# Edge means: TensorE reads a round's ten block numbers as two packed words of ready offsets

## The reference, cut to what matters

```python
count = zeros(N); total = zeros((N, 16))
count[dst] += 1                      # edges that arrive at each node
total[dst] += edge_attr_16           # their 16 attributes, summed
mean16 = total / maximum(count, 1)   # used by the second graph layer
dinv = 1 / sqrt(count + 1)           # used by the third graph layer
```

## Time and profile before

| what | value |
| --- | --- |
| time, median of 3 runs | 6425.63 us (6424.36 to 6426.48) |
| time of the profiled execution | 6432.7 us |
| its span | 6431.1 us |
| first to last read of block numbers in the stage | 1952.3 us to 2158.5 us of the span, 22 reads |
| granted TensorE clock, whole span | 0.899 |

### The profile page before, as it was taken

One profiled execution on the slowest core, in us unless ns is written; L12 is line 12 of the kernel. 1 busy time (PEld: TensorE's weight loads), 2 busy tenths in 40 slices (PEclk: granted clock), 3 DMA queues, 4 the chain that ended last, 5 costly groups with the idle time before them and its releaser, 6 DMA issues. The chain is left out here.

```text
span 6431.1 us, 120342 instructions
## 1 busy us (share of the span) xinstructions
PE 4931.8 (77%) x25586; PEld 3714.0 (58%) x25587; DVE 4307.1 (67%) x13252; ACT 2765.0 (43%) x8055; POOL 3078.3 (48%) x3493
## 2 busy tenths in 40 slices
PE   5621999994574578888883899969989997888685
PEld 4510777763453356666663566645657775666575
DVE  7770888873785679999996777753433335888612
ACT  0010877773114336666662111124523333877423
POOL 4786777776473048888880222213310001777221
PEclk9975999997695689999995999979999998999698
DMA  6522444455585222222231555543520002666453
GB/s 237 179 65 58 122 121 124 119 112 104 142 250 147 61 59 69 69 68 70 67 67 49 170 181 188 184 127 106 154 79 10 10 10 60 160 160 159 75 170 118
DMA packets 843340, 719.85 MB, mean 112 GB/s; under 512 B 405662, under 2 KB 749251, under 8 KB 842660
## 3 DMA queue, kind: packets, MB, share of 16 engines
q1 hardware_dynamic: 596280, 372.06, 20.3%
q0 software_dynamic: 120064, 280.26, 16.4%
q10 hardware_dynamic: 126828, 65.67, 3.5%
HBM read 521.19 MB, written 201.60 MB: 112 GB/s over the span
## 5 line engine op out<-in xcount | busy, mean ns | idle before, releaser
L1054 POOL DMA_INDIRECT l3e_rows<-table,l3e_idx x440 | 437.4, 994 | 736.6 <-DVE l3e_idx L1076 608.3
L1054 POOL DMA_INDIRECT l0e_rows<-table,l0e_idx x440 | 446.9, 1016 | 149.9 <-issue 132.0
L1054 POOL DMA_INDIRECT l1e_rows<-table,l1e_idx x440 | 429.1, 975 | 121.4 <-issue 121.4
L3366 ACT ACTIVATE l1e_weighted<-l1e_rows,l1e_power 128x64 f32<-128x64 f32 x1760 | 462.9, 334 | 16.7 <-ACT l1e_power L3357 9.3
L824 POOL DMA_INDIRECT records_by_src<-l0n_rec_src,l0n_pos_at_src x390 | 398.1, 1021 | 115.4 <-issue 108.8
L1331 PE MATMUL l0e_ps_w<-l0e_wf,l0e_hidT 128*128 128x256 f32 x1760 | 415.8, 390 | 34.5 <-DVE l0e_shifted L1272 34.3
L1331 PEld LDWEIGHTS l0e_ps_w<-l0e_wf,l0e_hidT 128*128 128x128 f32 x1760 | 330.3, 193 | 161.9 <-issue 88.4
L3307 PE MATMUL l1e_ps_row<-net_ident,l1e_logit 128*128 128x128 f32 x1760 | 276.9, 280 | 127.5 <-DVE l1e_logit L3502 126.4
L2673 ACT ACTIVATE l1fg_hT<-l1fg_ps_h,l1fg_b_cols 128x256 f32<-128x256 f32 x256 | 107.3, 470 | 530.6 <-PE l1fg_ps_h L2616 530.6
L2055 ACT ACTIVATE l2fe_hT<-l2fe_ps_h,l2fe_own,l2fe_own 128x320 f32<-128x320 f32 x320 | 197.5, 617 | 310.1 <-PE l2fe_ps_h L2005 309.8
L3321 PE MATMUL l3e_ps_s<-l3e_weighted,l3e_onehot 128*128 128x257 f32 x880 | 253.0, 433 | 93.0 <-ACT l3e_weighted L3368 92.9
(11 more groups left out here) (833 smaller groups left out, 14858.8 us busy)
## 6 DMA issues: line engine op xcount, KB each, us to landing
counts<-l1f_total ACTq DMA_DIRECT2D x272, 128.0 KB, 4.0
l1fg_w_in<-in_L_ffn_W SPq DMA_DIRECT2D x32, 1024.0 KB
l1fg_w_out<-in_L_ffn_W SPq DMA_DIRECT2D x32, 1024.0 KB
records_by_dst<-l0n_blank_dst SPq DMA_DIRECT2D x5, 6512.0 KB
l3e_rec<-records_by_dst SPq DMA_DIRECT2D x110, 296.0 KB, 3.2
l2d_counts<-counts SPq DMA_DIRECT2D x208, 128.0 KB, 2.4
l2d_counts<-counts POOLq DMA_DIRECT2D x192, 128.0 KB, 2.7
l3fg_w_in<-in_L_ffn_w SPq DMA_DIRECT2D x16, 1024.0 KB, 7.2
```

The lines of the kernel that those rows point to most:

```text
L1054: pool.indirect_dma_start(at(self.rows[b], k, self.width), None, self.table, bass.IndirectOffsetOnAxis(self.idx[b][:, k:k + 1], 0)).then_i ...
L3366: act.activation(out[:, h, 0:each], g.rows[b][:, lo:lo + each], ACT.Copy, scale=power[b][:, m * heads + h:m * heads + h + 1])
```

## The change

At the end of setup VectorE packs the block numbers five to a word, five bits each, and shifts each word left by six bits, so that a field read in place is already the number times 64, the column at which the block's sums begin. There are 44 such words, in `round_word_dst`. TensorE reads two words at the head of a round in place of ten numbers, tests the two against bounds, and takes each field out with a shift and a mask ahead of the pair's matmuls (with a mask alone for the first field of a word). The matmuls and their operands are the same.

```diff
+FIELDS, FIELD_BITS, SUMS_BITS = 5, 5, 6
...
+        self.round_word = None if weighted else s.sb(f"round_word_{key}", [P, PAIRS // FIELDS], I32)
...
         link(dve.tensor_copy(to.block_row[:, :], t["pair_blk"]))
+        word, fields = to.round_word[:, :], to.block_row[:, :].rearrange("p (w n) -> p w n", n=FIELDS)
+        link(dve.tensor_copy(word, fields[:, :, FIELDS - 1]))
+        for n in reversed(range(FIELDS - 1)):
+            link(dve.tensor_single_scalar(word, word, FIELD_BITS, op=ALU.logical_shift_left))
+            link(dve.tensor_tensor(word, word, fields[:, :, n], ALU.bitwise_or))
+        link(dve.tensor_single_scalar(word, word, SUMS_BITS, op=ALU.logical_shift_left))
...
-def blocks_of_round(net, engine, placed, first, n):
-
-    _, blocks = net.nc.values_load_multi_w_load_instructions(placed.block_row[0:1, bass.ds(first, n)], engines=[engine],
-                                                             min_val=0, max_val=NT - 1)
-    return blocks
+def offsets_of_round(net, engine, placed, rnd):
+
+    n = RING * TWO // FIELDS
+    top = ((NT - 1) * ((1 << FIELD_BITS * FIELDS) - 1) // ((1 << FIELD_BITS) - 1)) << SUMS_BITS
+    _, words = net.nc.values_load_multi_w_load_instructions(placed.round_word[0:1, bass.ds(rnd * n, n)], engines=[engine],
+                                                            min_val=0, max_val=top)
+    mask = ((1 << FIELD_BITS) - 1) << SUMS_BITS
+    return [(word >> (FIELD_BITS * m)) & mask for word in words for m in range(FIELDS)]
...
                 if b == 0:
-                    of_round[:] = blocks_of_round(net, mybir.EngineType.PE, placed, q * TWO, RING * TWO)
-                blocks = of_round[b * TWO:(b + 1) * TWO]
+                    of_round[:] = offsets_of_round(net, mybir.EngineType.PE, placed, i)
+                offsets = of_round[b * TWO:(b + 1) * TWO]
...
-                    pe.matmul(at(ps, blocks[k // 2], W)[:, 0:SUMS], at(onehot[b], k, P),
+                    pe.matmul(ps[:, bass.ds(offsets[k // 2], SUMS)], at(onehot[b], k, P),
```

More of the change, by code:

```diff
@@ L2941, in combine_and_means @@
     TILE = 16 + 9 * 16
-    SUMS, W = 49, 64
+    SUMS, W = 49, 1 << SUMS_BITS
     TWO_TILES = NT // 2
```

## The result

The median of four runs after is 6377.18 us (6372.94 to 6379.6), against 6426.06 us (6424.36 to 6437.09) for four runs before: a ratio of 0.9913, with an interval of 0.9901 to 0.9925. The forecast was 6368.5 us, with a range of 6358 to 6390. The profiled execution after took 6377.27 us, with a span of 6375.6 us and a granted clock of 0.902.

The account below looks back on a forecast made before the run. TensorE's sequencer at each round's head was taken as the bound. 21 rounds go from 206.2 to 9 × 6.9 + 12 × 7.05 = 146.7 us; less 0.9 and 1.5, net 57.1 off 6425.6 gives 6368.5 us, range 6358 to 6390.

Parts of the forecast that it names:

- The read: At TensorE's round head, reading two words in place of ten numbers takes 0.55 us, saving 1.33 us a round.
- The forecast's lower end: Lowest price for reading two words at the round's head: 0.30 us plus the short reads' slope of 0.09, 0.39 us.
- The tests: At TensorE's round head, eight fewer run-time bounds tests at 0.287 us each save 2.30 us a round.
- The register operations: On TensorE, 18 added operations a round to take out fields cost 93 ns each, 1.67 us a round.
- Rival 3: Operations taking out fields cost only 50 ns each; early rounds fall to SyncE's 6.3 us; 6362 us or less; chance 0.14.
- rival 4: Operations feeding a matmul's address cost more, turning point about 0.26 us each; at 0.30 us, 6446 us; chance 0.03.
- The round: TensorE's steps from start of sums to start of sums add to 6.79 us, 6.87 with the data chain.
- What is late next: After TensorE's head shrinks, the data chain sets early rounds at 6.9 us; VectorE's additions nearly set late ones, 7.05 us.
- VectorE's floor: In the last 12 rounds, VectorE's `last` steps and additions to `x` allow no round shorter than 6.96 us.
- The wait for the expert rows: Ten rounds in, VectorE waits for GpSimd's last fetch before its additions begin: +1.5 us once.
- Rival 2: Record loads into the stage become the limit, a round some 8 us: 36 us saved, 6390 us; chance 0.10.
- the first round: Filled by start-up, its read hidden but its register operations not wholly: +0.9 us once.

## Why the prediction was right, point by point

**The read.** 0.55 us forecast from "two times 0.27", 0.558 measured. The reason given was right for the wrong half: long reads do go word by word, at 0.27 us each (2.74 / 10). Short ones don't, and the runs show why: 0.85 us for twelve words is three steps of 0.28, and 1.08 for ten is two such steps and two single words, (2 + 2) × 0.27. An aligned read thus seems to take four words at a step and what is left one by one. Two words then make no group of four and go one by one from either address, which is why the forecast's price held: partly by luck, as it had the words of every read go so. Those three lengths and 0.30 for a single word fit this, and the 0.81 us expected for twelve words was worked out from it before the run; other lengths and other offsets weren't tried. The forecast's lower end, by the slope of the short reads, is not borne out. The Trainium skill ("Runtime: NRT & Kernel Launch", Instruction fetch mechanics) says about 200 ns a register, even in bulk. It says so of registers filled from HBM, and the reads here are of SBUF. The runs go from 0.07 us a word (twelve, aligned) to 0.27 (unaligned) and 0.30 (a single one), so its figure agrees here only with the mean over the kernel before, 0.19.

**The tests.** 0.287 us each: 2.30 us a round forecast for eight. In the changed kernel the two tests of a round still begin 0.286 us apart. The kernel without any of the ten shortened its rounds by 2.4 of 2.87 us, and there the late rounds with a short read stop at 6.82 us, near VectorE's own limit (below). Two tests fewer after the change took 0.5 of 0.57 us off the early rounds. The price stands.

**The register operations.** 0.093 us forecast, 0.096 in the trace, 0.07 to 0.09 as what ten more added. The same section of the Trainium skill names an issue floor of some 20 cycles an instruction, an estimated 17 ns at the prediction's 1.2 GHz. The row of 32 to 36 ns alone is twice that. A floor is a lower bound and no price, so the trace does not contradict it, as the prediction had it do. Rival 3 (50 ns each) is out, as is rival 4 (0.26 us).

**The round.** Term by term: head 2.63 forecast and 2.63 measured, then 1.12 and 1.11, 1.01 and 1.12, 0.92 and 0.98, 1.11 and 1.11. The sum was 6.87 and is 6.95; the mean of the early rounds is 7.05. That two terms agree to the last digit is luck in part: six neighbouring heads take 2.62 to 2.77 us.

**What is late next.** 7.05 us was forecast for late rounds and 7.08 measured, but "VectorE's floor, 4 × 0.99 + 3.00 = 6.96" was put together wrongly. The 0.99 was itself set by TensorE and ScalarE. Where VectorE has a backlog its step is 0.95 (2031.41 to 2032.36, 2033.30). In a late round of both kernels with ready offsets the five steps of `last` are 0.96, three of 0.94 and 2.98, 6.76 us in all, with nothing left to wait for: that is VectorE's floor. In most late rounds of the changed kernel they are some 0.96, 0.94, 1.03, 1.17 and 2.99, so VectorE waits ahead of two of them. The 7.08 is a longer loop, seen in this stretch of the changed kernel:

```profile
2071.86 2.12 DVE L3113 SCALAR_TENSOR_TENSOR net_x<-means_out,l0f_weight,net_x  x4
...
2073.91 0.29 DVE L3106 TENSOR_TENSOR means_parts<-means_rest,means_parts 128x128 bf16<-128x128 f32 x1
...
2074.63 0.47 PE L3050 MATMUL means_ps<-means_parts,means_onehot 128*128 128x49 bf16 x4
...
2075.58 0.60 PE L3050 MATMUL means_ps<-means_parts,means_onehot 128*128 128x49 bf16 x4
...
2076.87 0.60 ACT L3080 ACTIVATE means_partsT<-means_ps_t 128x512 bf16<-128x512 bf16 x1
...
2077.36 0.35 ACT L3069 ACTIVATE means_parts<-means_rec 128x192 bf16<-128x192 f32 x1
2077.62 0.35 ACT L3073 ACTIVATE means_parts<-means_rest 128x192 bf16<-128x192 f32 x1
...
2078.00 0.29 DVE L3106 TENSOR_TENSOR means_parts<-means_rest,means_parts 128x128 bf16<-128x128 f32 x1
...
2078.95 0.48 DVE L3113 SCALAR_TENSOR_TENSOR net_x<-means_out,l0f_weight,net_x  x1
```

VectorE's additions make `last` late (2073.91); TensorE's third batch waits for it, and does this and the next batch with their register operations (2074.63, 2075.58); its transposes release ScalarE's `keep` (2076.87), behind which stand `first` and `second`; these release `last` (2078.00), and one `hot` later the next additions begin. The loop passes two batches of TensorE but not the round's head. It is read from these rows, and three runs bear it out: removing the head's tests leaves 7.08, taking the register operations away gives 6.76, and moving the additions gives TensorE's own 6.95. With ten more register operations TensorE's own round, 6.95 + 10 × 0.093 = 7.88 us, is the longer of the two limits again, against 7.78 measured.

**Once only.** The wait for the expert rows was to cost 1.5 us; it cost 1.6 in the profiled run and 3.6 in the next. It is the term with the largest scatter. GpSimd's last fetch was issued 67.0 us after the first in the profiled run and 69.4 in the next, where it was 65.3 before. The kernels with aligned and with shifted rows, whose rounds are longer, took 71.6 and 67.4 us on that chip, so the difference is not shown to come from the change. The two stretches of the earlier trace rows in the changed kernel:

```profile
1967.40:2030.40 63.00, 44.55 (x360) 26.49 (x360) 45.68 (x133) 47.14 (x136) 47.31 (x45) 0.52 0.90 216
2030.40:2120.20 89.80, 63.38 (x505) 38.00 (x506) 81.91 (x234) 65.99 (x184) 0.00 (x0) 0.50 0.53 120
```

The DMA share in the early rounds is 0.90, where it was 0.61, with 216 GB/s for 147. Rival 2 had this for a limit. VectorE's wait for the records grew only from 2.7 us to 4.4, and ScalarE's from 11.3 to 11.8, so it did not take hold. It may be what makes the early rounds 7.05 us and not 6.95: on the third chip, where the fetches end before the third round and the share is 0.56 behind it, the early rounds take 6.93. No run on one chip separates this. TensorE's granted clock is 0.52 and 0.50, the 1.2 GHz level, as before.

**The miss.** 57.1 us were forecast, and the medians differ by 48.9 (by 49.7 against the 16 runs on the first chip). Inside the stage, first and last read came 53.3 us closer. The term that was mis-sized is the first round. The sum counts it among the nine rounds of 6.9 us and adds 0.9, 7.8 us in all. It took 10.1 us before and takes 9.98 after, and the prediction's own working of the expert rows has it at 9.8 + 0.9. That is 2.2 us; the eight early rounds at 7.05 make 1.2 us, the late ones 0.3, the round of the wait 0.1. Behind the last read the stage's end gave 2.0 us more, and its start took 0.3, which leaves the 54.9 us of the stage. One sign did not follow from the sum, either: 206.2 - 57.1 is 149.1 us from first to last read, and "155 to 158" was written. 152.9 was measured, between the two.

The other 6 us lie outside the stage, of which the forecast said that nothing changes but the shift. Three things are seen there in the traces of the six executions that took 6371 to 6445 us and, for the first, of all the others.

- Behind the stage, line 1139 (1149 in the changed kernel) has 220 single reads. First and last are 1062.7 us apart before, and 1061.6 to 1064.1 in the six other runs that pack nothing, on all three chips. They are 1064.5 and 1064.7 us apart in the two executions of the changed kernel, and 1064.9 to 1065.4 in four others that pack (1063.2 in the one with the additions at the end). Some 2 us are lost there; why isn't known.
- Ahead of it, VectorE's first operation after setup starts at 612.4 us before and after, so the ten new operations cost nothing there, as forecast. From it to the stage's first read pass 1339.9 us before and 1340.3 without the tests, but 1343.5 to 1347.8 in the four executions with a new tensor in SBUF (the changed kernel twice, aligned and shifted rows). 4.3 us of that are scatter between two executions of the changed kernel; whether the rest belongs to the change is open.
- The execution that was profiled before was 7 us above its median. Its last part, from the third such operation at 5429.7 us, took 1001.4 us, against 996.6 to 999.4 in the five others.

So the step that carried most of the error is taking the stage's saving, read off one profiled execution, for the kernel's. The cover of the setup is a matter of the chip, too: on the second and third chip VectorE's last operation there ends some 3 us before the next begins, in place of 134. No trace of the kernel before exists there to show what the ten operations cost.

**The other signs.** TensorE's gap at a round's head is 1.6 to 1.7 us (1.9 forecast), ScalarE's wait for TensorE 38.9 us (45), and VectorE is busy for 81.9 of the last 89.8 us, 91%, where it was 70%.

## What to carry to other kernels

Price what a sequencer does at a loop's head, since no engine's busy time shows it: here a run-time bounds test of 0.287 us, times ten, was worth more than any other part, and dropping it alone gave most of the gain. Where a kernel reads several numbers into registers, try rows padded to whole groups of four words that begin at multiples of 16 bytes: here alignment alone gave 0.2%, and together with offsets made ready and no tests it did as well as packing. When a stall is removed, look for the loop across engines that comes next and ask which of your instructions it passes: shortening those outside it gives nothing.

## What the runs showed of the hardware that was not expected

- A read of ten int32 words into TensorE's registers takes from 1.07 us (median 1.09 to 1.25) from a multiple of 16 bytes and 2.74 us in the median from 8 bytes past one; twelve words, aligned, take from 0.85 us (median 0.88).
- A run-time bounds test of one register takes 0.287 us on TensorE's sequencer, and a register operation about 0.09 us with its gap.
- The same program takes 6429 us on one chip and 7273 or 7263 us on two others, at a granted clock of about 0.87 there against 0.90. In the changed kernel on the first and third chip, 220 of the 840 us lie ahead of 612 us of the first chip's trace, 399 between there and 2253 us, 3 in the next 3125 us and 219 behind. Some stages with indirect DMAs are longer, as are two or three rounds at the start of this stage (9 to 60 us while GpSimd fetches), but one with 440 indirect DMAs takes 1057 us on both. The late rounds agree to 0.01 us (7.08). Why was not looked into.
